# The matrix engine's share of a quantised attention: its six middle head pairs written out or run as a loop

## The reference, cut to what matters

```python
attn = jnp.einsum('bhqd,bhkd->bhqk', q, k)
attn = jax.nn.softmax(attn.astype(jnp.float32), axis=-1)
attn = _fq_unsigned(attn, axis=-1)      # round(attn / s), s = row maximum / 255
out = jnp.einsum('bhqk,bhkd->bhqd', attn, v)
```

## Time and profile before

| | |
|---|---|
| time, median of 3 runs | 2947.03 us (2945.35 to 2948.09) |
| the profiled execution | 2948.09 us, of which the profile's span is 2946.2 us |
| keys and values | 82 to 1409 us |
| quantised attention, first score to last | 1457 to 2153 us |
| instructions in the span | 42369, of PE 16808 products and 16808 weight loads |
| granted TensorE clock, mean | 0.959 |

### The profile page before, as it was taken

One profiled execution on the slowest core, in us unless ns is written; L12 is line 12 of the kernel. 1 busy time (PEld: TensorE's weight loads), 2 busy tenths in 40 slices (PEclk: granted clock), 3 DMA queues, 4 the chain that ended last, 5 costly groups with the idle time before them and its releaser, 6 DMA issues. The chain is left out here.

```text
span 2946.2 us, 42369 instructions
## 1 busy us (share of the span) xinstructions
PE 2612.4 (89%) x16808; PEld 1327.1 (45%) x16808; DVE 1860.9 (63%) x2883; ACT 1033.5 (35%) x920; POOL 553.9 (19%) x208
## 2 busy tenths in 40 slices
PE   6999999999999999999377777777759999499998
PEld 3444444444444444444144444444444476244443
DVE  5855555555555555554489999999944343566663
ACT  3111111111111111111189999999962133211100
POOL 0500000000000000000256546645610721011100
PEclk9999999999999999999689999999989977699999
DMA  6121222212221222212479999999871300300000
GB/s 236 65 79 57 78 85 78 72 67 81 85 78 57 78 85 78 72 67 68 122 172 180 194 208 185 194 199 197 176 224 60 112 1 1 61 15 15 8 0 29
DMA packets 493040, 288.93 MB, mean 98 GB/s; under 512 B 403200, under 2 KB 468992, under 8 KB 488064
## 3 DMA queue, kind: packets, MB, share of 16 engines
q1 hardware_dynamic: 492928, 287.28, 37.5%
HBM read 117.37 MB, written 69.21 MB: 63 GB/s over the span
## 5 line engine op out<-in xcount | busy, mean ns | idle before, releaser
L456 PE MATMUL kv_acc<-kv_whi,kv_xthi 128*128 128x512 f16 x2048 | 776.8, 379 | 5.6 <-DVE kv_xtlo L500 5.6
L456 PE MATMUL kv_acc<-kv_wlo,kv_xthi 128*128 128x512 f16 x2048 | 776.7, 379 | 0.0
L456 PE MATMUL kv_acc<-kv_whi,kv_xtlo 128*128 128x512 f16 x2048 | 776.7, 379 | 0.0
L919 DVE TENSOR_SCALAR_CACHE_REDUCE at_sc<-at_score 128x1024 f32<-128x1024 f32 x512 | 612.0, 1220 | 47.8 <-PE at_score L812 43.4
L1005 ACT ACTIVATE at_sc<-at_sc,at_bias,at_qs 128x4096 uint16<-128x4096 f32 x128 | 484.8, 3791 | 13.4 <-DVE at_bias L931 13.4
L812 PE MATMUL at_score<-at_kt,at_q 128*128 128x512 f16 x1024 | 309.2, 392 | 88.0 <-DVE at_sc L919 43.1
L487 ACT ACTIVATE kv_parts<-kv_key 128x1024 f16<-128x1024 f32 x64 | 67.6, 1057 | 866.6 <-DVE kv_key L525 866.6
L456 PEld LDWEIGHTS kv_acc<-kv_whi,kv_xthi 128*128 128x128 f16 x2048 | 200.5, 98 | 247.9 <-DVE kv_xtlo L500 6.1
L456 PEld LDWEIGHTS kv_acc<-kv_whi,kv_xtlo 128*128 128x128 f16 x2048 | 200.5, 98 | 242.0 <-issue 0.8
L456 PEld LDWEIGHTS kv_acc<-kv_wlo,kv_xthi 128*128 128x128 f16 x2048 | 200.5, 98 | 241.8 <-issue 0.6
L506 DVE SCALAR_TENSOR_TENSOR kv_key<-kv_acc,kv_bias 128x512 f32<-128x512 f32 x128 | 88.5, 692 | 335.1 <-PE kv_acc L456 335.1
(11 more groups left out here) (181 smaller groups left out, 3285.0 us busy)
## 6 DMA issues: line engine op xcount, KB each, us to landing
kv_rows<-in_ctx SPq DMA_DIRECT2D x64, 512.0 KB, 6.0
key_rows<-kv_parts SPq DMA_DIRECT2D x64, 512.0 KB, 2.6
values<-kv_val SPq DMA_DIRECT2D x32, 1024.0 KB, 6.3
x<-values SPq DMA_DIRECT2D x16, 2048.0 KB, 8.8
wq_stage<-in_wkv SPq DMA_DIRECT2D x4, 2048.0 KB, 7.8
x<-in_x SPq DMA_DIRECT2D x2, 2048.0 KB, 8.2
wq_stage<-in_wq SPq DMA_DIRECT2D x2, 2048.0 KB, 13.1
wt_stage<-in_wp SPq DMA_DIRECT2D x2, 2048.0 KB, 10.1
```

The source lines that it names most:

```text
L456: last = nc.tensor.matmul(acc[c][:], a[s][:, k, :], b[:, c, k, :], start=(k == 0 and q == 0), stop=(k == KD - 1 and q == 2))
L919: nc.vector.tensor_scalar(sc[n % 2][:, c * SC:(c + 1) * SC], score[pos % 2][:], 1.0, None, ALU.mult, ALU.max, accum_out=part_max[n % 2][:, ...
```

## The change

PE's eight calls become the same `each_pair` as on the other engines. Pair 0, pair 7, the prologue and the final `finish_slot` calls stay as they were. Pairs 1 to 6 become one body in a loop: it is passed six times, and the branch back to its head is taken five times. In the body each semaphore count that depends on `i` is worked out in a register (`h * CH + pos - 1`, `EXP0 + 2 * g + 2`, and so on) instead of being a constant.

```diff
             inputs_ready(0, 0)
             for c in range(CH + AHEAD):
                 scores(c // CH, c // CH, c % CH)
-            for i in range(PAIRS):
-                body(i, i == 0, i == PAIRS - 1)
+            each_pair(pe, body)
             for c in range(CH):
                 finish_slot(PAIRS, 0, c)
```

## The result

The changed kernel takes 2981.38 us (median of 4 runs, 2978.23 to 2982.23), the kernel before 2946.19 us beside it: a ratio of 1.0117, 95% interval 1.0101 to 1.0133, so 35.2 us or 1.2% slower. The profiled execution took 2982.49 us, with a span of 2980.6 us, 34.4 us more than that of before.

The account below looks back on a forecast made before the run. DVE was taken to set the pace of quantised attention, with 0.53 us idle a pair; 0 + 0 + 5 x 3.1 + 0 = 15.6 us on 2947.0 gave 2962.6 us, range 2945 to 2976.

Parts of the forecast that it names:

- Work and instruction traffic: In the attention stage, unchanged products and loads, and seven instruction packets a pair, 0.5% of the DMA engines: 0 us.
- The fetch: At each of five taken edges PE waits for the body's head to be brought in: 5.1 us, bounds 1.8 and 7.2.
- The cover: At each edge, queued products and idle time (1.46 us) plus DVE's slack (0.52 us) hide 1.98 us, or 1.26.
- Registers: 900 waits on PE in six pairs take counts from registers: 0 us, hidden in PE's waiting, at most 5.7 us.
- The branch with its target at hand: Five taken branches at the pair edges, without any fetch: 0 us, at most 0.3 us.
- Stays resident: Rival: PE's whole attention loop body is kept, nothing is fetched in pairs 2 to 6, 2947 us; chance 0.24.
- The Trainium skill's 2048 instructions: PE's instruction memory of 128 KiB, by which a body of about 1,900 would just fit and the sum be 0.
- The Trainium skill's rule of a two-page window: A taken branch with its target outside the current two-page window forces a fetch, so each of five edges pays.
- Registers gate the scores: Rival: register additions on PE delay scores beyond the slack, evenly in every slot, 5.7 us, 2953 us; chance 0.04.
- The sum of the bounds: Upper limit for the whole change: five edges at 5.9 us plus 5.7 us for register waits, 35.4 us.
- the edges' bound: Upper limit for the five taken edges: 5.9 us each, a fetch of 7.2 us less 1.26 us covered.

Follow-up runs that it names:

- the first experiment: Kernel before with PE's pairs 1 to 6 written out but the pair number in a register, no loop: 2950.30 us against 2947.94, ratio 1.0009.
- the thin kernel: Kernel before, written out, with 30 of the 32 `dma_sums` products left out in each slot: 2937.05 us against 2947.74 for the kernel before.
- the thin loop: Changed kernel with 30 of the 32 `dma_sums` products left out in each slot: 2938.10 us against 2947.74 for the kernel before.
- the shifted run: Changed kernel with 96 already satisfied waits ahead of the stage, moving the loop's body within its packets: 2988.70 us against 2945.84, ratio 1.0145.
- that with the hint: Changed kernel with a branch prefetch hint at the head of each pass of the loop: 2975.92 us against 2947.94, ratio 1.0094.
- the run with all three edits: Changed kernel with loop cut after a pair's second chunk, 96 instructions added ahead, and two waits before a slot's first turns swapped: 2977.59 us against 2945.84, ratio 1.0106.
- the run without the added waits: Changed kernel with loop cut after a pair's second chunk and two waits before a slot's first turns swapped: 2969.71 us against 2947.74, ratio 1.0076.

## Why the prediction was wrong

The direction, the mechanism and the place were right: five edges, the first score late for DVE, instruction packets in every pass. The size was 15.6 us where 35.2 were measured. By its steps:

*Work and instruction traffic: 0.* Right. Three packets more a pass showed nowhere but at the edge.

*The fetch: 5.1 us.* It took 6.2 us from the queued loads to the next (branch records 6.03 to 6.22), inside the bounds of 1.8 and 7.2. Mis-sized by 1.1 us an edge, 5.5 us in all. The row I took it from was that of other transfers. By the packets' records two start together at these edges, about 2.0 us after the branch, and have come 3.5 to 4.2 us after it; what fills the 2 us until the branch ends, no run shows. In the runs where one packet starts at that point, the branch lasts 4.2 to 5.0 us.

*The cover: 1.98 us.* Right. 6.20 - 1.98 = 4.22 us, and 0.43 for the slow score, is 4.65; DVE's row says 4.66.

*The clock: no term.* This is the step that failed by omission, and the largest single miss. I let PE stand idle and then run on as before. It came back at half speed, 0.43 us on the first score and 1.13 us on the second, 1.56 us an edge and 7.8 us in all, and more at the fifth edge. The expected idle time of PE was not weighed against the clock row at all.

*Registers: 0, bound 5.7 us.* Wrong, 3.6 us. The reason given was that a score may be 0.52 us late. That holds for the score at the edge, not for that of the next chunk, which stands behind 16 transposes that start when the exponentials end: it is complete 0.03 us before DVE copies it, as the first experiment's rows show. In that chain 0.075 us a slot count in full. With it a premise falls, that DVE alone sets the pace and PE can give back no more than 0.53 us a pair; the thin kernel gave back 1.25.

*The branch with its target at hand: 0.* Right, twice: 1,577 instructions in keys and values, and the thin loop in attention.

15.6 + 5.5 + 7.8 + 3.6 = 32.5 us, against 32.2 us by which the stage grew from first score to last. The closeness is partly luck, as said above: the fifth edge cost more and the first pair less.

*The rivals.* "Stays resident" was decided against this body, and its condition was the right one: everything that fits stays. The Trainium skill's 2048 instructions ("Runtime: NRT & Kernel Launch", "Instruction fetch mechanics"), read as in the prediction, would have let a body of 1,914 stay; the trace doesn't agree, it fetches 10 packets a pass. Read as eight whole packets, the figure isn't refuted: 1,914 instructions lie across eight or nine packets, and one more comes in than the body touches (17 a pass for a body of about 3,820, which touches at most 16). No run lies between 1,577 and 1,914. The Trainium skill's rule of a two-page window, in the same section, does not hold here: 1,577 instructions, six packets' worth, stayed. "Registers gate the scores" was true besides, evenly in every slot as described, at 3.6 us. The sum of the bounds, 35.4 us, would have held the result, but by luck: its 5.9 us an edge come from a fetch of 7.2 us less a cover of 1.26, and neither occurred. The range stopped short at 2976 us, the edges' bound with nothing for the registers. And causes come together here: a long fetch brings the idle time, and the idle time the clock.

## What to carry to other kernels

Before a long written-out program of one engine becomes a loop, count its instructions: up to about 1,580 on PE the taken branch cost nothing here, at 1,914 it cost 4.0 to 7.6 us in attention. If it has to be too long, put the branch where the products queued behind it last as long as the fetch; 3.5 us of them made it free on DMA engines 23% busy. Don't take an engine's small idle time for the most that its partner can win or lose: look for the work that it starts the moment the partner delivers. Where a wait ends last in a chain, let the instruction itself carry it, with the register work and the satisfied waits ahead.

## What the runs showed of the hardware

- PE loop bodies of 1,433 and 1,577 instructions were not fetched again, bodies of 1,914 and 1,971 in each pass, with 10 packets of 16 KB (9 in the shifted run and in that with the hint) for 7.5 to 7.7 packets' worth.
- A taken branch on PE lasted 0.21 us with its target kept, 3.3 to 3.8 us with a fetch on DMA engines 23% busy, and 4.2 to 6.2 us at about 94%.
- The granted clock fell from 1.00 to 0.50 within a stall of PE of 5.36 us, and the products after it ran at half speed (16 transposes 1.91 us instead of 1.07). In the run with all three edits it fell at a stall of 3.99 us and not at 3.83; in the run without the added waits it fell at 3.67 us.
- A wait whose count is in a register cost nothing on the weight load, and 0.075 us when it sat on a register operation ahead of it.
